# Products with values for four exponent steps at a time, and the first maximum behind h in four of eight slots

## The reference, cut to what matters

```python
qkv = x @ Wqkv + bqkv                       # q: 16 heads, k and v: 4 groups, used by 4 heads each
scores = einsum('bqhd,bkhd->bhqk', q, k) / HD
prob = softmax(scores)
out = einsum('bhqk,bkhd->bqhd', prob, v)    # "products with values" below
x = layernorm(x + out @ Wout + bout)
gate, up = split(x @ ternary(w_gate_up))
h = silu(gate) * up
x = layernorm(x + rms_norm(h) @ ternary(w_proj))
```

## Time and profile before

| | us |
|---|---|
| median of 3 runs | 569.85 (569.84 to 571.31) |
| the profiled execution | 570.28 |
| its span, first to last instruction | 568.3 |

### The profile page before, as it was taken

How to read it: one execution, slowest core, us unless ns; L and a number is a source line. 1 busy time by engine, 2 the same in 40 slices (tenths; PEclk the granted TensorE clock), 3 DMA queues, 4 the chain that set the end, 5 groups by cost and what they waited for, 6 DMA issues and landing times.

```text
span 568.3 us, 13548 instructions
## 1 busy us (share of the span) xinstructions
PE 524.5 (92%) x4148; PEld 444.7 (78%) x4148; DVE 442.4 (78%) x1002; ACT 366.0 (64%) x738; POOL 335.5 (59%) x517
## 2 busy tenths in 40 slices
PE   4687999899999999999999999999999999999883
PEld 4677778688888888888888888888888888777772
DVE  6876796868888897878787888888888878775764
ACT  4553765466676777676767667676767675667663
POOL 4566764245556656574756656556556565656764
PEclk9896999999999999999999999999999999999998
DMA  8867163536162626354454535262627062010001
GB/s 227 140 142 123 56 125 76 104 71 110 52 116 60 125 30 145 54 126 73 105 96 100 96 89 107 74 115 63 119 37 155 10 152 48 21 40 1 19 20 37
DMA packets 83379, 49.16 MB, mean 86 GB/s; under 512 B 39680, under 2 KB 83328, under 8 KB 83328
## 3 DMA queue, kind: packets, MB, share of 16 engines
q1 hardware_dynamic: 81584, 48.00, 41.0%
q10 hardware_dynamic: 1744, 0.53, 0.4%
HBM read 33.29 MB, written 14.68 MB: 84 GB/s over the span
## 4 chain that ended last, share of the span: by engine, by line
PE 47%; POOL 19%; issue 15%; DVE 10%; ACT 3%; DMA 3%; SPq 1%; ACTq 1%; POOLq 0%; DVEq 0%
PE ffn_ps L588 12%; PE short_ps L514 8%; PE pv_ps L616 7%; PE short_ps L560 6%; PE exp_ps L569 5%; PE down_ps L601 5%; POOL sq_sum L1015 5%; POOL h_lo L1010 4%; POOL rstd L999 2%; DVE row_max L834 2%; DVE h_f L910 2%; DVE gated L903 2%; POOL attB L403 1%; POOL k_p L1034 1%; DMA q_st<-shift_lo 1%
## 5 line engine op out<-in xcount | busy, mean ns | idle before, releaser
L834 DVE TENSOR_REDUCE row_max<-short_ps 128x2 f32<-128x512 f32 x256 | 174.0, 682 | 60.6 <-PE short_ps L560 60.0
L1010 POOL TENSOR_TENSOR h_lo<-h_f,h_hi 128x256 fp32r<-128x256 f32 x128 | 94.5, 739 | 179.7 <-ACT h_hi L737 179.5
L761 ACT ACTIVATE probs<-exp_ps 128x1024 f32<-128x1024 f32 x128 | 130.7, 1021 | 44.5 <-PE exp_ps L569 43.9
L560 PE MATMUL short_ps<-k_st,q_st 65*128 65x256 f32 x512 | 108.5, 296 | 3.6 <-DVE row_max L834 3.3
L746 ACT ACTIVATE tanh<-ffn_ps 128x256 f32<-128x256 f32 x120 | 45.7, 381 | 96.9 <-PE ffn_ps L588 96.9
L560 PEld LDWEIGHTS short_ps<-k_st,q_st 65*128 65x128 f32 x512 | 88.5, 193 | 15.1 <-issue 2.4
L588 PE MATMUL ffn_ps<-x1T_hi,wguT 128*128 128x256 f32 x480 | 80.8, 291 | 9.9 <-DVE h_f L910 9.3
L569 PE MATMUL exp_ps<-q_st,k_st 67*128 67x512 f32 x256 | 81.6, 400 | 3.3 <-DMA q_st<-shift_lo 3.2
L601 PE MATMUL down_ps<-wpT,h_hi 128*128 128x256 f32 x256 | 79.2, 332 | 3.7 <-POOL h_lo L1010 3.5
L588 PE MATMUL ffn_ps<-x1T_lo,wguT 128*128 128x256 f32 x480 | 78.0, 285 | 0.2 <-DVE x1T_lo L823 0.2
L588 PEld LDWEIGHTS ffn_ps<-x1T_hi,wguT 128*128 128x128 f32 x480 | 65.1, 189 | 16.0 <-issue 10.9
(11 more groups left out here) (104 smaller groups left out, 831.2 us busy)
## 6 DMA issues: line engine op xcount, KB each, us to landing
q_st<-q_dram SPq DMA_DIRECT2D x128, 128.0 KB, 4.1
q_dram<-q_p SPq DMA_DIRECT2D x16, 512.0 KB, 3.0
k_st<-k_dram SPq DMA_DIRECT2D x64, 64.0 KB, 2.3
res<-in_L_attn_x_dram SPq DMA_DIRECT2D x16, 256.0 KB, 2.9
out_dram<-y_out SPq DMA_DIRECT2D x16, 256.0 KB, 2.9
xn<-in_L_attn_x_dram SPq DMA_DIRECT2D x62, 64.0 KB, 2.6
wgu_raw<-in_L_ffn_w_gate_up_dram SPq DMA_DIRECT2D x8, 256.0 KB, 6.4
k_dram<-k_p SPq DMA_DIRECT2D x16, 128.0 KB, 2.6
```

What stands on the lines that cost most here:

```text
L560: last = pe.matmul(bank[:, t * S:(t + 1) * S], q_st[0:PAD, st.par, head, t * P:(t + 1) * P], k_st[0:PAD, st.par, st.s % 4, :], start=True, ...
L761: act.activation(probs[:, st.s % 4], exp_ps[:], ACT.Exp).then_inc(exp_done, 1)
L834: dve.tensor_reduce(row_max[:, st.par, head * TT:(head + 1) * TT], short(n, f"max{i}")[:].rearrange("p (t k) -> p t k", t=TT), AX.X, ALU.m ...
L1010: pool.tensor_tensor(h_p[1][:, st.s % 4, :], h_f[:, st.s % 2, :], h_p[0][:, st.s % 4, :].bitcast(F32), ALU.subtract).then_inc(h_lo, 1)
```

## The change

Four things. `times_v` runs once for four exponent steps instead of once for two: in slots 3 and 7, with sixteen products, instead of slots 1, 3, 5 and 7 with eight. `probs` holds eight steps, and all waits that count these products count two a sequence instead of four. To make room, eight tiles of the feed-forward stage (tanh, gated, h and others) become slices of `wgu_raw`, which holds the raw weights at the start of the run. And in slots 0, 1, 5 and 6 DVE takes the first maximum behind `h_f` instead of ahead of `gated`; in slots 2, 3, 4 and 7 it stays where it was.

```diff
+MAX_BEHIND = (0, 1, 5, 6)
...
-        probs = sb("probs", [P, 4, TT, 2, S])
+        probs = sb("probs", [P, SLOTS, TT, 2, S])
...
+        tanh, gated, h_f, h_sq, y_sb, r2, y_even, y_odd = (wgu_raw[:, 2 * i:2 * i + 2, :] for i in range(8))
+        y_out = (y_even, y_odd)
...
-                if st.s % 4 == 1:
-                    wait(pe, pv_turned, st.count(2, st.s // 4))
-                for t in range(TT):
-                    for s in (st.s - 1, st.s):
-                        for i in range(2):
-                            r = 32 * quadrant(s % 4, i)
-                            last = pe.matmul(pv_ps[r:r + 32, s % 4 // 2, :], v_ones[:, st.par, t, s % 4, :],
-                                             probs[:, s % 4, t, i, :], start=(t == 0), stop=(t == TT - 1),
-                                             tile_position=(0, r))
+                wait(pe, pv_turned, st.count(2, st.s // 4))
+                for first in (st.s - 3, st.s - 1):
+                    for t in range(TT):
+                        for s in (first, first + 1):
+                            for i in range(2):
+                                r = 32 * quadrant(s % 4, i)
+                                last = pe.matmul(pv_ps[r:r + 32, s % 4 // 2, :], v_ones[:, st.par, t, s % 4, :],
+                                                 probs[:, s, t, i, :], start=(t == 0), stop=(t == TT - 1),
+                                                 tile_position=(0, r))
                 last.then_inc(pv_done, 1)
...
-                if (st := n.chunk(PV0)) and st.s % 2:
+                if (st := n.chunk(PV0)) and st.s % 4 == 3:
                     times_v(st)
...
-                    wait(act, pv_done, st.count(4, st.s // 2 - 1))
-                    act.activation(probs[:, st.s % 4], exp_ps[:], ACT.Exp).then_inc(exp_done, 1)
+                    wait(act, pv_done, st.count(2, st.s // 4 - 1))
+                    act.activation(probs[:, st.s], exp_ps[:], ACT.Exp).then_inc(exp_done, 1)
...
             def slot(n):
-                if st := n.chunk(MAX0):
+                if (st := n.chunk(MAX0)) and n.t % SLOTS not in MAX_BEHIND:
                     take_maximum(n, st, 0)
...
                     dve.tensor_tensor(h_f[:, st.s % 2, :], gated[:, st.s % 2, :], gate_up_bank(n, st, 0), ALU.mult
                                       ).then_inc(h_done, 1)
+                if (st := n.chunk(MAX0)) and n.t % SLOTS in MAX_BEHIND:
+                    take_maximum(n, st, 0)
                 if st := n.once(SHIFT_SPLIT[0]):
                     shift_rows(n, st, 0)
```

More of the change, by code:

```diff
@@ L295, in postln_layer @@
         x1T = [sb(f"x1T_{n}", [P, 2, DT, S], F32R) for n in ("hi", "lo")]
-        tanh = sb("tanh", [P, 2, S])
-        gated = sb("gated", [P, 2, S])
-        h_f = sb("h_f", [P, 2, S])
+        tanh, gated, h_f, h_sq, y_sb, r2, y_even, y_odd = (wgu_raw[:, 2 * i:2 * i + 2, :] for i in range(8))
+        y_out = (y_even, y_odd)
         h_p = [sb(f"h_{n}", [P, 4, S], F32R) for n in ("hi", "lo")]
-        h_sq = sb("h_sq", [P, 2, S])
         sq_sum = sb("sq_sum", [P, 2, S])
-        y_sb = sb("y_sb", [P, TT, D])
         ms = sb("ms", [P, TT])
         inv = sb("inv", [P, TT])
-        r2 = sb("r2", [P, TT, D])
         st2 = sb("st2", [P, TT, 6])
@@ L311, in postln_layer @@
         mean2 = sb("mean2", [P, TT])
-        y_out = sb("y_out", [P, 2, TT, D])
         exp_ps = ps("exp_ps", [P, TT, 2 * S])
@@ L487, in slot @@
                     sp_wait(y_done, st.count(TT, TT))
-                    sp.dma_start(out[st.seq()].rearrange("(t p) d -> p t d", p=P), y_out[:, st.par]
+                    sp.dma_start(out[st.seq()].rearrange("(t p) d -> p t d", p=P), y_out[st.par]
                                  ).then_inc(stored[st.par], 16)
@@ L751, in slot @@
                     for t in range(TT):
-                        act.activation(y_out[:, st.par, t, :], r2[:, t, :], ACT.Identity, bias=shift2[:, t:t + 1],
+                        act.activation(y_out[st.par][:, t, :], r2[:, t, :], ACT.Identity, bias=shift2[:, t:t + 1],
                                        scale=rstd2[:, t:t + 1]).then_inc(y_done, 1)
@@ L940, in slot @@
                     if st := n.once(PV_NORM[half]):
-                        wait(dve, pv_done, st.count(4, 2 * half + 2))
+                        wait(dve, pv_done, st.count(2, half + 1))
                         wait(dve, att_done, st.count(2, half))
@@ L959, in slot @@
                     wait(dve, v_made, st.count(1, 1))
-                    wait(dve, pv_done, st.count(4, -4))
+                    wait(dve, pv_done, st.count(2, -2))
                     v = short(n, "v")[:, 0:TT * P].rearrange("p (t r g d) -> p t r g d", t=TT, r=2, g=G)
```

## The result

The changed kernel takes 596.58 us (median of 4 runs, 596.24 to 597.62), the kernel before 569.85 (of 4 runs, too, 569.20 to 571.31): a ratio of 1.0472, 95% interval 1.0449 to 1.0494. It was forecast at 590, between 574 and 597. The profiled execution took 596.71 us for a span of 594.5.

What follows compares the result with a forecast made beforehand. PE was taken to set the pace in mid-run, with short slots bound by the chain through h. Thirteen periods of +1.57 us gave +20.4, fill and tail 0: profiled 570.28 to 590.7, median 590, range 574 to 597.

Steps and rivals of the forecast that it cites:

- Four more rounds cost 0.85; the call lasts 1.85: Merged `times_v` on PE: four added rounds at 0.21 us cost 0.85, so a merged pair saves 0.15 us or more.
- Slots 0 and 1: T2 = T0 + 5.74: From slot 0's `gate_up` start (T0) to slot 2's (T2): 5.74 us, before 6.61, a gain of 0.87.
- Slot 2: max0 waits for the second maximum of slot 1 and starts at T0 + 6.94; T3 = T0 + 11.82: PE waits 0.25 us for bank 2 in slot 2; slot 3 starts at 11.82, before 12.44, leaving 0.62 gain.
- Slot 5: tanh 2.05, x1 turn held by the maximum, T6 = T5 + 4.34: Tanh keeps its time in slot 5; the x1 turn waits for the maximum's bank, making the slot 0.40 us longer.
- Slot 6 and 7: second half of `gate_up` 3.76 after slot 6's first: Slot 7's second half of `gate_up` waits for `x1T_lo` behind the maximum: 3.76 us against 3.67, 0.09 later.
- A period +1.57: Slots 0 to 2 −0.62, slot 3 +0.85, slot 5 +0.40, slot 6 +0.09, slot 7 +0.85; 13 periods, +20.4 us.
- The clock stays: PE's granted clock was not expected to fall; the rival that it does, about 655 us, had chance 0.01.
- The rival in which PE stays the bound, 559 us: Each of 32 merges gives 0.15 us and slot 6's 0.40 wait goes 16 times; faster, 559 to 567: chance 0.11.
- The range: Whole kernel: 574 to 597 us, leaving out the faster cases and the clock; 583 to 597 by the mechanism, chance 0.78.
- fill and tail, taken as 0 of bounds −3 and +3: Ahead of slot 31 and behind slot 134: 0 us, bounds three calls' worth of 1.00 saved or 0.85 added.

Runs made afterwards that it cites:

- grouping alone: Changed kernel with every first maximum back ahead of gated, four-step calls, eight-step `probs` and moved tiles kept: 588.25 us, ratio to the kernel before 1.0310.
- the order alone: Kernel before, products still in pairs, with only the first maximum behind h in slots 0, 1, 5 and 6: 575.72 us, ratio 1.0094.
- 6 to 8: Kernel before with maximum behind h and `x1T_lo` moved up in slot 6; then also slot 0's maximum; then also early mean square: 565.63, 565.58, 563.86 us.

## Why the prediction was right, and by how much it missed

The direction and the mechanism were right. By its own steps:

- *Four more rounds cost 0.85; the call lasts 1.85.* 381.51 − 377.07 against 3.58 gives +0.86 for slot 3, and the call that begins at 379.07 has its next one, `down`, 1.87 later. A merge saves about 0.14 us by starts, 0.21 of busy time; 0.15 or more was said.
- *Slots 0 and 1: T2 = T0 + 5.74.* Measured 370.90 − 365.13 = 5.77. Tanh of slot 1 came 4.42 after T0, forecast 4.41.
- *Slot 2: max0 waits for the second maximum of slot 1 and starts at T0 + 6.94; T3 = T0 + 11.82.* Measured 6.97 and 11.94. The wait for the maximum is there, at the weight load (0.19 us; 0.25 was forecast). Of the gain of 0.87 some 0.50 was left, where 0.62 was forecast.
- *Slot 5: tanh 2.05, x1 turn held by the maximum, T6 = T5 + 4.34.* Tanh 2.05; turn 3.99 after `gate_up`; T6 = T5 + 4.40. The 0.74 from the maximum's start to the product behind it, carried over from `x1T_lo`, is 0.74 here, too. The turn itself takes 0.41 rather than the 0.35 that was carried over from before.
- *Slot 6 and 7: second half of `gate_up` 3.76 after slot 6's first.* From 389.15 to 392.19 + 0.74 it is 3.78.
- *A period +1.57.* The 13 periods gave +21.5 us instead of +20.4, but by two errors of opposite sign. The ten from slot 47 to slot 127 gave +1.80 each, short by 2.25 us in all: 0.12 of a period in slots 0 to 2, 0.06 in slot 5, a few hundredths in slots 3, 6 and 7. The first two of the 13 and the last gave +0.87, +1.39 and +1.30, together 1.15 less than was counted for them. The run is less regular than the prediction read it: of the seven periods averaged to 30.18 the last is 29.35, the others 30.22 to 30.40.
- *The clock stays.* The granted clock of the ten periods is 1.00, with PE busy 300.92 of 321.03 us. "TensorE: Matmul & The Clock Gate" of the Trainium skill says, in its section on a second HAM failure mode, that short idle stretches between groups of products can make the clock swing: no swing is in these rows.
- *The rival in which PE stays the bound, 559 us.* It was to be decided by the turn of slot 5; that waits, 13 times, 16.7 us in all. The drain that "TensorEngine Tiling (Array Packing)" of the Trainium skill names in Key Properties is consistent with the 0.14 us that a merge saved, but no run separated it from the other costs of a call.
- *The range.* Its lower end, 583, was put to a period of +1.0 without the waits of slot 2; by the prediction's own terms that is −1.00 + 0.85 + 0.40 + 0.09 + 0.85 = +1.19, about 585. Its upper end, 597, was put to slots 0 to 2 giving back almost nothing, which is not what happened. That 596.58 stayed 0.4 us inside it is in part luck.

**The step that was mis-sized is the last one: fill and tail, taken as 0 of bounds −3 and +3.** They came to +4.7. The tail is the larger part, and the starts of `gate_up` show it. Changed kernel: slots 135, 136, 139, 140 and 144:

```profile
518.81 0.71 PE L587 MATMUL ffn_ps<-x1T_hi,wguT 128*128 128x256 f32 x4
...
523.98 0.64 PE L587 MATMUL ffn_ps<-x1T_hi,wguT 128*128 128x256 f32 x4
...
534.99 0.71 PE L587 MATMUL ffn_ps<-x1T_hi,wguT 128*128 128x256 f32 x4 [0.77 <-DVE wgu_raw L909]
...
539.01 0.64 PE L587 MATMUL ffn_ps<-x1T_hi,wguT 128*128 128x256 f32 x4
...
550.80 0.64 PE L587 MATMUL exp_ps<-x1T_hi,wguT 128*128 128x256 f32 x4
```

Kernel before: slots 136, 139, 140 and 144 (slot 135 starts at 495.58):

```profile
499.28 0.64 PE L588 MATMUL ffn_ps<-x1T_hi,wguT 128*128 128x256 f32 x4
...
510.29 0.71 PE L588 MATMUL ffn_ps<-x1T_hi,wguT 128*128 128x256 f32 x4 [0.76 <-DVE h_f L910]
...
513.45 0.64 PE L588 MATMUL ffn_ps<-x1T_hi,wguT 128*128 128x256 f32 x4
...
524.91 0.64 PE L588 MATMUL exp_ps<-x1T_hi,wguT 128*128 128x256 f32 x4
```

From slot 135 to slot 144 it is 550.80 − 518.81 = 31.99 us after, 524.91 − 495.58 = 29.33 before: as much as a period and a half, +2.66 of the +3.0. Slot 135 has +1.47 of it (5.17, before 3.70), slot 139 +0.86 (4.02, before 3.16), slot 143 as much (3.55, before 2.69); the slots between give 0.53 back. I had counted the periods up to slot 134, but merged calls stand in slots 135, 139 and 143 too, and slots 3 and 7 pay for them as they do in the middle of the run. The bound of +3 was made of just such calls; I took the middle of the range instead of the end that the mechanism points to. The split of the tail by parts of the change: it is 74.9 us with grouping alone and 73.9 with the order alone, 75.7 with both, 72.7 before.

The fill's +1.7 is not shown to be an effect of the change. 1.0 of it is there at the first scores of slot 9 (30.41 us, before 29.40), ahead of all products with values, and these scores start anywhere between 28.77 and 32.03 us in the profiled runs of the experiments' kernels. Slot 31 starts between 100.94 and 104.73 us there: at 100.94, 102.32 and 103.63 in the three with pairs of 6 to 8. The span was to grow by 20.4 us and grew by 26.2; the 1.1 us of this miss that the fill and tail do not explain is the period, as said above.

## What to carry to other kernels

Before work of the busiest engine is collected into fewer, cheaper calls, ask in each place it leaves what it covered, and in each place it joins whether that place is bound by the same engine: saved busy time turned into idle time here, and the added rounds counted in full. An instruction that is moved behind a release also moves every release of its own; look up in the same stage who waits for its bank, and who for the output behind it. A change that slows each period is paid until the last of the affected work is done, not until the steady part ends.

## What the runs showed of the hardware that was not expected

- A product call of fp32 with 32 columns of weights, run as one of eight rounds instead of two of four, held PE for 1.86 or 1.87 us instead of 2 × 1.00, and still no kernel with it was faster. The busy time of its rows fell by more, 0.21 us a merge, because rows overlap: the starts give the price.
- Eight added products in an idle stretch cost nothing that can be measured: 594.93 us against 596.58, ten periods in 321.02 us against 321.03 with PE busy 9.6 us longer, slot 5 at 4.41 in both.
- The first maximum's order in slot 6 alone, with `x1T_lo` moved up, was worth 0.9% of the kernel before (ratio 0.9913, 0.9884 to 0.9941).
